# Eight extra matmuls ahead of each turning of edge records, in the graph layers of a GNN and feed-forward kernel

## The reference, cut to what matters

```
ew = edge_attr @ edge_w + edge_b                 # 100000 x 32 by 32 x 256
for l in range(3):
    msg = relu(x[src] * ew)
    for i in range(3):                           # the edge's type
        h = segment_sum(msg * mask[i], dst) / count[i]
        out += h @ weights[l, i]
    x = x + relu(out + x @ roots[l] + biases[l])
```

## Time and profile before

| | |
|---|---|
| median of 3 runs | 8658.48 us (8642.5 to 8659.21) |
| profiled execution | 8648.77 us |
| its span, first to last instruction | 8646.9 us |
| mean granted TensorE clock | 0.774 of full |
| TensorE busy | 5543.5 us, 64% |
| VectorE busy | 4711.0 us, 54% |
| GpSimd busy | 4308.0 us, 50% |
| ScalarE busy | 2517.1 us, 29% |

### The profile page before, as it was taken

One profiled execution on the slowest core, in us unless ns is written; L12 is line 12 of the kernel. 1 busy time (PEld: TensorE's weight loads), 2 busy tenths in 40 slices (PEclk: granted clock), 3 DMA queues, 4 the chain that ended last, 5 costly groups with the idle time before them and its releaser, 6 DMA issues.

```text
span 8646.9 us, 127794 instructions
## 1 busy us (share of the span) xinstructions
PE 5543.5 (64%) x26499; PEld 3762.6 (44%) x26499; DVE 4711.0 (54%) x11031; ACT 2517.1 (29%) x5780; POOL 4308.0 (50%) x4197
## 2 busy tenths in 40 slices
PE   6699322223777778466666686666767666666678
PEld 2355111111444444344454564444545544554465
DVE  7777555555555457544454554444545445554563
ACT  0388111111444442122222232222223222222231
POOL 0000676776777772455555525555553355555500
PEclk9999555555887888677777887777778777787889
DMA  4000566666555540333333333333334233333420
GB/s 132 16 0 0 177 211 206 211 208 176 130 130 132 126 126 24 106 88 89 89 96 88 92 51 92 90 88 93 95 92 68 71 88 94 91 95 93 91 36 21
DMA packets 426891, 865.07 MB, mean 100 GB/s; under 512 B 114194, under 2 KB 246648, under 8 KB 426663
## 3 DMA queue, kind: packets, MB, share of 16 engines
q0 software_dynamic: 200448, 465.27, 21.0%
q1 hardware_dynamic: 179210, 253.37, 9.4%
q10 hardware_dynamic: 47136, 145.32, 5.9%
HBM read 671.12 MB, written 191.23 MB: 100 GB/s over the span
## 4 chain that ended last, share of the span: by engine, by line
PE 30%; another core or an unknown queue 11%; issue 7%; DVE 5%; DVEq 5%; DMA 0%; POOL 0%; ACT 0%; SPq 0%; ACTq 0%; POOLq 0%
PE bank L1026 15%; PE bank L1071 3%; DVEq L1435 3%; PE bank L1038 3%; PE bank L1039 2%; PE bank L1040 2%; DVE z_mem L1608 2%; DVE acc_mem L1435 2%; DVEq L1425 2%; PE bank L1016 1%; PE bank L972 1%; PE bank L982 1%; PE bank L1061 1%; DVE z_mem L1598 1%
## 5 line engine op out<-in xcount | busy, mean ns | idle before, releaser
L1435 DVE TENSOR_TENSOR acc_mem<-acc_mem,bank 128x257 f32 x3376 | 1424.4, 422 | 2069.0 <-remote 794.8
L1026 PE MATMUL bank<-z_mem 128*128 128x257 f32 x5136 | 1681.9, 477 | 416.1 <-DVE z_mem L1598 166.8
L508 POOL DMA_INDIRECT sort_mem<-x_d,x_mem x1296 | 1246.2, 962 | 1075.5 <-issue 399.7
L508 POOL DMA_INDIRECT x_mem<-x_d,x_mem x1272 | 1227.5, 965 | 894.2 <-issue 442.5
L1038 PE MATMUL bank<-z_mem 99*128 99x256 bf16 x2568 | 806.7, 314 | 1103.1 <-DVE z_mem L1608 673.3
L1026 PEld LDWEIGHTS bank<-z_mem 128*128 128x128 f32 x5136 | 1134.3, 237 | 735.3 <-issue 350.7
L465 POOL DMA_INDIRECT acc_mem<-h_d,z_mem x808 | 839.0, 1038 | 888.8 <-ACTq L600 619.8
L725 ACT ACTIVATE z_mem<-bank 99x512 bf16<-99x512 bf16 x642 | 383.1, 597 | 2657.9 <-remote 2051.9
L481 POOL DMA_INDIRECT recB_d<-sort_mem x800 | 958.4, 1198 | 273.7 <-issue 273.7
L735 ACT ACTIVATE z_mem<-z_mem 128x512 f32<-128x512 f32 x1284 | 808.2, 630 | 716.8 <-DVE z_mem L1608 441.8
L1038 PEld LDWEIGHTS bank<-z_mem 99*128 99x128 bf16 x2568 | 278.7, 109 | 1392.1 <-DVE z_mem L1608 752.5
(11 more groups left out here) (272 smaller groups left out, 7091.2 us busy)
## 6 DMA issues: line engine op xcount, KB each, us to landing
pay_d<-acc_mem SPq DMA_DIRECT2D x202, 516.0 KB
acc_mem<-pay_d ACTq DMA_DIRECT2D x202, 516.0 KB
x_mem<-recB_d SPq DMA_DIRECT2D x642, 104.0 KB
sort_mem<-x_d,x_mem POOLq DMA_INDIRECT x1296
x_mem<-x_d,x_mem POOLq DMA_INDIRECT x1272
edge_d<-xnt_mem ACTq DMA_DIRECT2D x40, 507.8 KB
sort_mem<-edge_d SPq DMA_DIRECT2D x40, 507.8 KB
recB_d<-acc_mem SPq DMA_DIRECT2D x3, 5616.0 KB, 33.6
```

The lines of the kernel that those rows point to most:

```text
L508: pool.indirect_dma_start(out=xg[h % XG][:, k, :], out_offset=None, in_=x_d, in_offset=bass.IndirectOffsetOnAxis(ap=reci[h][:, k, W_SRC:W_ ...
L1026: m.matmul(bank[4 + k][:, :AC], oneh[:, h, k, :], msg[:, h, k, :], start=True, stop=True)\
L1435: v.tensor_tensor(a_, a_, bank[banks + k][:, :AC], ALU.add).then_inc(flushed, 1)
```

## The change

Ahead of the four transposes of each quad, TensorE issues eight more bf16 matmuls. The stationary operand is `ident_b` cut to 99 rows, the moving one the first part of the edge weights, 256 columns. They write columns 256 to 511 of the bank whose first half the transposes write; nothing reads those columns, and nothing waits for the eight. They stand behind the wait for the copy of the quad before (which also covers the earlier reading of this bank) and ahead of the wait for the records.

```diff
                 def turn(Q, h, n):
                     if due(Q - 1):
                         pe.wait_ge(S("attr_ready"), l * QB + Q - 1)
+                    for _ in range(8):
+                        m.matmul(bank[h % 2][:, 256:512], ident_b[:KA, :], we[:KA, 0, :], start=True, stop=True)
                     pe.wait_ge(S(f"fed{h}"), fed_before(l, h) + n * 16 + 16)
                     for k in range(4):
                         last = m.transpose(bank[h % 2][:KA, 0:256].bitcast(BF16)[:, k * P:(k + 1) * P],
```

## The result

| | before | after |
|---|---|---|
| median | 8658.84 us (8642.50 to 8677.96, 4 runs) | 8801.98 us (8763.42 to 8834.68, 4 runs) |
| profiled execution, its span | 8648.77, 8646.9 us | 8825.58, 8823.7 us |
| mean granted clock of the span | 0.774 | 0.805 |
| three layers, first to last copy of turned records | 4450.5 us | 4622.7 us |

The ratio is 1.0151, with a 95% interval of 1.0117 to 1.0184: the change costs 1.5%. The profiled execution grew by 177 us, and 172 of these are in the layers.

A forecast was written before the change was run, and what follows sets the result against it. The prediction took waiting for TensorE results that become known late while gathers are issued to bound the layers, no engine being full. Terms +198, +40 and -120 made +118 us on 8648.8: forecast 8770 us, range 8430 to 9010.

The forecast's parts named there:

- The state of the kernel before: Layers: no engine needs the 6.95 us a quad; TensorE's results become known late while gathers are issued.
- Extra at half clock, +198: Burst in the layers' half-clock quads: 193 quads x 1.71 us = 330 us, x 0.6 on the path, +198 us.
- Extra at full clock, +40: Burst in 449 full-clock quads: VectorE's 4.23 us round covers all but 0.2 us; +40 us, 237 without cover.
- The old work at a better clock, -120: Layers' existing TensorE work: half clock falls from 45% to 30%, mean clock 0.85, saving 200 us, x 0.6: -120 us.
- rival 1: Layers: burst keeps the clock up and more than pays for itself; faster, 8480 us, chance 0.34.
- The path share of 0.6: Layers, TensorE: 0.6 of the burst's time lies on the path, taken from 45% and 62% of quads by the chain.
- Instruction fetch: TensorE's layer loop body grows by 128 instructions; by rule a fetch stall each turn, by rows none; left out of sum.
- Rival 2: Layers: clock doesn't move, half clock stays at 45%, burst is pure cost; +338 us, 8987 us, chance 0.10.
- Rival 3: Layers: burst runs hidden while results are late anyway, clock's gain small; within 17 us of 8650, chance 0.09.
- What I said would show it: 5136 matmuls at 0.11 and 0.21 us, layers' clock 0.85 and 1525 us each, long waits kept, other stages unmoved.

The follow-up runs named there:

- plain: Kernel before with the layers' four indirect gathers a quad replaced by plain DMAs of fixed contiguous rows, no extra matmuls: 6863.39 us beside 8654.01.
- half_plain: Kernel before with two of a quad's four indirect gathers in the layers replaced by plain DMAs of fixed rows: 6890.16 us beside 8676.48.
- plain8: Kernel with the eight extra matmuls, all four indirect gathers a quad in the layers replaced by plain DMAs of fixed rows: 6874.19 us beside 8654.01 for before.
- tiny8: Changed kernel with its eight extra matmuls a quad cut from 256 to 16 columns each: 8861.22 us beside 8654.01 for before, ratio 1.0226.
- wide4: Changed kernel with four extra matmuls of 512 columns ahead of a quad's first sum instead of its eight: 8744.90 us beside 8676.48 for before, ratio 1.0082.
- n16: Changed kernel with sixteen extra matmuls a quad instead of eight, same place: 9081.37 us beside 8694.68 for before, ratio 1.0449.
- paced: Kernel before, no extra matmuls, gathers at most four quads ahead instead of eight: 7219.14 us, ratio 1.000, on a third chip where before took 7218.15.

## Why the prediction was right, and where only its sum was

The forecast was 8770 us, the median 8802. By steps:

**The state of the kernel before.** Right: no engine bounds the layers, late results do (on the chips on which the change was timed). plain and half_plain show it by taking the gathers away. But I wrote that results become known late *while gathers are issued*, as if the gathers were enough. The third chip shows that they are not. Nor is it only TensorE's results, as the stages ahead of the layers show.

**Extra at half clock, +198.** The layers' clock is 0.837, so half clock holds 0.33 of the time, against the 0.30 forecast: 209 quads x 1.71 = 358 us of streaming. With the quotient of 0.47 in place of 0.6: +168.

**Extra at full clock, +40.** This was too small. 433 quads x 0.88 = 381 us. I let VectorE's round of 4.23 us cover most of it. plain8 shows that this cover is real where VectorE's round sets the pace (21 us in 642 quads). But a late quad takes far longer than 4.23 us, and what follows the late result is, as I read it, a chain that TensorE's work is part of. At the same quotient it is +179 us. I even had the uncovered size in the text, 237, as the case of the cover gone, and didn't weigh it against the fact that quads take 6.95 us.

**The old work at a better clock, -120.** The clock came as forecast, 0.84 against 0.85. Streaming saved is 358 + 381 - 366 (the net growth) = 373 us, where I had 200; at 0.47 it is -175. This 373 is too high, since busy time hides what went into gaps. Counted from the starts of the rows instead (each up to the next start, at most its spacing at half clock), the old matmuls take 2832 us before and 2538 after and the burst 722: 294 us saved and a net growth of 428, of which the layers' 172 are 0.40. At 0.40 the three terms are +143, +152 and -118, so by this count the clock's term came as forecast. The share of products at half clock fell from 28 to 15%.

Together 168 + 179 - 175 = +172, which is what the layers grew by since 0.47 is read from it. How the three divide is my reckoning with one quotient for all, not a measurement; tiny8 (0.95) and wide4 (0.20) speak against one quotient for bursts of other make. So the full-clock term was 112 to 139 us too small by either count, and the first term was 30 to 55 us too dear (the third by up to 55), which brought the sum to within 54 us of the layers' growth. The direction and the clock were understood, the full-clock term was not. That 8770 lies as near to 8802 as it does is in part luck: errors in opposite directions, and tiny8, which has almost none of the streaming that the sum counts and no gain of clock, costs as much as the full burst. The sum has no term for that.

One row was read too generously for rival 1: the products and sums are 44% of the chain in the stretch shown in the earlier trace rows, not 47% (that is with the transposes), and so not its larger part.

**The path share of 0.6.** What can be measured is the quotient, 0.45 to 0.60 for bursts of this form at any of the numbers and places tried. 6% of the span for L1015 in the chain is 529 us of 739 of streaming, 0.7, so the chain counts more than the time pays.

**Instruction fetch.** The larger queue shows 42 packets against 37. The Trainium skill, "Runtime: NRT & Kernel Launch", "Instruction fetch mechanics", would have a stall at every turn of a body that outgrew the loaded code. With some 72 turns and five packets more, the body isn't fetched anew at each turn, and n16, whose body is longer still, shows 48 packets and keeps the quotient (0.50).

**Rival 1, the clock pays for it all.** The clock rose by 28% of the distance to full, and the time rose too. Long waits stand as before, as at 6305.67. The Trainium skill, "TensorE: Matmul & The Clock Gate", "Why this matters for your kernels", asks for no idle gaps between bursts. The runs agree that more streaming lifts the clock (0.77 to 0.87 with sixteen), and they show that filler in front of or behind the work, with the gaps left as they are, costs more than it gives back. **Rival 2** (no rise) would have needed 0.78. **Rival 3** (all hidden) is what plain8 does, in a kernel without late results, though not for the reason that rival 3 gave, which was the late results.

**What I said would show it.** The 5136 matmuls at 0.11 us and the clock of 0.84 (0.85 forecast) came, and the layers take 1541 us on average (1525 forecast); the other stages grew by 177 - 172 = 5 us. The long waits stayed, and those of VectorE's additions grew.

**What stays open.** Why results come late on some chips (not even whether it is the chip or its condition at the time); whether pacing the gathers helps there (not tried there); why tiny matmuls cost as much as full ones, and so whether the 1.5% is the price of the burst's length or of its instructions; and what the change does on a chip like the third. By plain8, TensorE's 4.2 us would fit under GpSimd's 5.0, so I would expect next to nothing, but it wasn't run. The 1.5% holds for the chips on which before takes 8.65 ms.

## What to carry to other kernels

Filler matmuls stand ahead of what others wait for. At none of the three places and in none of the counts and sizes tried did the higher clock pay for them, and for bursts of the full form about half of TensorE's net growth ended up in the time. Ask of each term whether its cover is what sets the pace: VectorE's round of 4.2 us hid the burst in plain8 and didn't in a kernel whose quads take 7. Where a profile shows long waits with no named releaser, take away the suspected partner (here the indirect gathers, 1800 us of 8650) before adding anything elsewhere, and run the unchanged kernel on more than one chip.

## What the runs showed of the hardware that I had not expected

- The same kernel took 7218 us on one chip (13 runs within 0.25%) and 8618 to 8722 us on two others, 1216 of the 1429 us between the profiled executions in the layers (4450.5 against 3234.2 us, the latter by paced). In the layers on the slower chips ScalarE copied a quad's transposes 10.5 us after they had started (6371.69 before) against 0.5 us on the third, its longest unnamed wait was 36.0 us, and the clock was 0.77 against 0.98. The waits outside the layers, such as the 231 us of L887, are gone on the third chip as well.
- On the slower chips, two plain DMAs in place of two of four indirect ones per quad took the time from 8676 to 6890 us; all four replaced took it from 8654 to 6863.
- Eight matmuls of 16 columns, 0.20 us on TensorE, cost 2.3% (1.7 to 2.8), at least about as much as eight of 256 columns, 0.87 us or more (1.5%, 1.2 to 1.8).
- An fp32 matmul of 257 columns is two rows in the trace, 0.22 us apart at full clock: eight rows for four matmuls, 1.96 us with the tail at 6303.33.
